# Adding x by an accumulating DMA to rows filled with b_up, four raw slots, and rewritten engine orders, in a role-switched adapter with layer norm

## What is computed

```python
h = einsum('bsh,bhk->bsk', x, W_down[role]) + b_down[role][:, None, :]
h = gelu(h, approximate=False)
u = einsum('bsk,bkh->bsh', h, W_up[role]) + b_up[role][:, None, :]
y = x + u
mean = y.mean(-1, keepdims=True)
var = ((y - mean) ** 2).mean(-1, keepdims=True)
out = (y - mean) * rsqrt(var + 1e-5) * gamma[role][:, None, :] + beta[role][:, None, :]
```

## Time and profile before

| | us |
|---|---|
| three runs | 407.95, 413.99, 415.98 |
| median of the runs | 413.99 |
| span of the profiled execution, first to last instruction | 407.0 |
| busy in it: PE, DVE, ACT, POOL | 369.9, 312.0, 193.2, 163.5 |
| mean granted TensorE clock in it | 0.954 |

### The profile page before, as it was taken

How to read it: one execution, slowest core, us unless ns; L and a number is a source line. 1 busy time by engine, 2 the same in 40 slices (tenths; PEclk the granted TensorE clock), 3 DMA queues, 4 the chain that set the end, 5 groups by cost and what they waited for, 6 DMA issues and landing times.

```text
span 407.0 us, 5068 instructions
## 1 busy us (share of the span) xinstructions
PE 369.9 (91%) x1548; PEld 298.2 (73%) x1548; DVE 312.0 (77%) x262; ACT 193.2 (47%) x358; POOL 163.5 (40%) x138
## 2 busy tenths in 40 slices
PE   6969879988999799997999979997999959999992
PEld 2748668866888678886888868886788848888881
DVE  1899298889776996959877897769969695694475
ACT  3459434584353733565343942637335652353332
POOL 0830195247330863217621473307532164328221
PEclk8799989998999989998999989999899988999998
DMA  6489902698128862399326991287813985244022
GB/s 196 169 306 376 387 16 105 201 394 331 56 103 304 324 248 99 131 330 335 136 103 203 324 392 61 103 294 279 303 75 135 333 263 225 94 157 163 0 103 104
DMA packets 23489, 84.05 MB, mean 206 GB/s; under 512 B 2741, under 2 KB 2741, under 8 KB 23477
## 3 DMA queue, kind: packets, MB, share of 16 engines
q1 hardware_dynamic: 23480, 83.94, 56.4%
HBM read 67.15 MB, written 16.78 MB: 206 GB/s over the span
## 4 chain that ended last, share of the span: by engine, by line
PE 54%; DVE 16%; issue 8%; ACT 8%; DMA 7%; POOL 4%; SPq 1%; ACTq 0%; DVEq 0%; POOLq 0%
PE up_ps L279 32%; PE down_ps L271 22%; DVE wd_lo L485 4%; DVE h_lo L555 4%; DVE x_lo L480 4%; ACT x_hi L349 3%; ACT h_full L408 2%; POOL rows L449 2%; DMA x_stage<-xT 2%; DMA rows<-x 2%; DMA wu_stage<-W_up 2%; DVE rows L497 2%; DMA wd_stage<-W_down 1%; ACT squares L368 1%; DVE rows L526 1%
## 5 line engine op out<-in xcount | busy, mean ns | idle before, releaser
L449 POOL TENSOR_TENSOR rows<-rows,b_up_all 128x1024 f32<-128x1024 f32 x32 | 89.8, 2823 | 135.0 <-DMA rows<-x 109.5
L279 PE MATMUL up_ps<-wu_hi,h_hi 128*128 128x512 f32 x256 | 85.6, 415 | 20.8 <-DVE h_lo L555 16.8
L271 PE MATMUL down_ps<-x_hi,wd_hi 128*128 128x512 f32 x256 | 83.4, 397 | 7.3 <-DVE wd_lo L485 3.5
L279 PE MATMUL up_ps<-wu_lo,h_hi 128*128 128x512 f32 x256 | 83.2, 405 | 0.0
L279 PE MATMUL up_ps<-wu_hi,h_lo 128*128 128x512 f32 x256 | 83.0, 404 | 0.0
L271 PE MATMUL down_ps<-x_lo,wd_hi 128*128 128x512 f32 x256 | 82.3, 393 | 0.0
L271 PE MATMUL down_ps<-x_hi,wd_lo 128*128 128x512 f32 x256 | 81.4, 389 | 0.0
L279 PEld LDWEIGHTS up_ps<-wu_hi,h_hi 128*128 128x128 f32 x256 | 50.2, 200 | 35.2 <-issue 20.9
L480 DVE TENSOR_TENSOR x_lo<-x_stage,x_hi 128x1024 fp32r<-128x1024 f32 x32 | 60.2, 1882 | 9.5 <-ACT x_hi L349 9.5
L497 DVE SCALAR_TENSOR_TENSOR rows<-up_ps,rows 128x1024 f32<-128x1024 f32 x31 | 37.9, 1222 | 37.4 <-PE up_ps L279 29.7
L271 PEld LDWEIGHTS down_ps<-x_hi,wd_hi 128*128 128x128 f32 x256 | 48.6, 191 | 19.2 <-issue 6.8
(11 more groups left out here) (36 smaller groups left out, 288.4 us busy)
## 6 DMA issues: line engine op xcount, KB each, us to landing
x_stage<-xT SPq DMA_DIRECT2D x32, 512.0 KB, 5.8
wu_stage<-W_up SPq DMA_DIRECT2D x32, 512.0 KB, 8.3
rows<-x SPq DMA_DIRECT2D x32, 512.0 KB, 7.7
wd_stage<-W_down SPq DMA_DIRECT2D x31, 512.0 KB, 6.0
out<-rows SPq DMA_DIRECT2D x31, 512.0 KB, 2.6
wd_stage<-W_down SPq DMA_DIRECT2D x2, 256.0 KB, 5.5
out<-rows SPq DMA_DIRECT2D x2, 256.0 KB, 2.0
roles_sb<-roles SPq DMA_DIRECT2D x1, 0.0 KB
```

Of the source, the lines that this page charges most:

```text
L271: return pe.matmul(down_ps[:, kc, :], wd_part[:, n, c * K + kc * P:c * K + (kc + 1) * P], x_part[:, n, c * S:(c + 1) * S], start=start, st ...
L279: mm = pe.matmul(up_ps[:, t % 2, half], h_part[:, kc, t * P:(t + 1) * P], wu_part[:, kc, half], start=(kc == 0 and h_part is h_hi and wu_p ...
L449: pool.tensor_tensor(rows[:, t, :], rows[:, t, :], b_up_all[:, bass.ds(role * H, H)], ALU.add).then_inc(biased, 1)
```

## The change

- `x_stage` and `wd_stage` get a slot for each of the four parts, with a semaphore for each slot. A part of batch b + 1 can be loaded as soon as the same part of batch b is split.
- The first chunk of x is loaded and rounded apart, as the first chunk of W_down was.
- The roles and b_down are loaded from ScalarE's queue instead of SP's.
- b_up, gamma and beta are no longer kept for all roles. In each batch SP fills `rows[:, t, :]` with the role's row of b_up (one DRAM row read for 128 partitions, 512 KB written), four times, and loads `gamma_row` and `beta_row` in the same way.
- x is added to the filled rows by a DMA with `accum_op=ALU.add`, issued by POOL after the fill has landed. The add on POOL and its semaphore `biased` are gone.
- The last tile of a batch is summed, centred, finished and stored at the beginning of the next batch; SP, ScalarE, POOL and VectorE have new orders.
- ScalarE takes the squares of a tile in one instruction, except for the very last tile, and POOL makes rstd in two operations.
- TensorE waits for `summed` one tile less far ahead at t = 0.

The core of the diff:

```diff
-        x_stage = sb("x_stage", [P, NSTAGE, CPL * S], F32)
-        wd_stage = sb("wd_stage", [P, NSTAGE, CPL * K], F32)
+        x_stage = sb("x_stage", [P, NLOAD, CPL * S], F32)
+        wd_stage = sb("wd_stage", [P, NLOAD, CPL * K], F32)
...
+            def load_next_part(b, next_role, i):
+                sp.wait_ge(x_split, NLOAD * b + i + 1)
+                load_x_part(b + 1, i)
+                sp.wait_ge(wd_split, NLOAD * b + i + 1)
+                load_wd_part(next_role, i)
...
+            def fill_rows(b, t, role):
+
+                if not is_first(b):
+                    sp.wait_ge(stored[t], 16 * b)
+                sp.dma_start(rows[:, t, :], b_up[bass.ds(role, 1), :].partition_broadcast(P)).then_inc(b_up_in_rows[t], 16)
+
+            def load_role_row(row, param, role, landed):
+                sp.dma_start(row[:, :], param[bass.ds(role, 1), :].partition_broadcast(P)).then_inc(landed, 16)
...
             def steps(b):
                 first, last = is_first(b), is_last(b)
+                role = load_role(sp, b)
                 if not last:
                     next_role = load_role(sp, b + 1)
...
+                    load_next_part(b, next_role, 0)
+                fill_rows(b, 0, role)
+                fill_rows(b, 1, role)
+                if not first:
+                    store(b - 1, NT - 1)
+                fill_rows(b, 2, role)
+                load_role_row(gamma_row, gamma, role, gamma_landed)
+                load_role_row(beta_row, beta, role, beta_landed)
+                fill_rows(b, 3, role)
                 if not last:
+                    for i in range(1, NLOAD):
+                        load_next_part(b, next_role, i)
                     for i in range(KC):
                         sp.wait_ge(wu_split, KC * b + i + 1)
                         load_wu_part(next_role, i)
...
+                for t in range(NT - 1):
+                    store(b, t)
...
@@ block.tensor @@
                     if t < 2:
                         if not first:
-                            pe.wait_ge(summed, NT * b)
+                            pe.wait_ge(summed, NT * b - 2 + t + 1)
...
@@ block.scalar, steps @@
                 if not first:
+                    variance(b - 1, NT - 1)
                     act.wait_ge(up_ready, NT * b)
...
+                round_wu(b)
+                gelu(b, 0, role)
                 if not last:
...
+                    round_next_part(b, 0)
+                gelu(b, 1, role)
+                gelu(b, 2, role)
+                gelu(b, 3, role)
+                if not last:
+                    round_next_part(b, 1)
+                    round_next_part(b, 2)
+                variance(b, 0)
+                if not last:
+                    round_next_part(b, 3)
+                variance(b, 1)
+                variance(b, 2)
...
@@ block.gpsimd @@
-                    pool.tensor_tensor(rows[:, t, :], rows[:, t, :], b_up_all[:, bass.ds(role * H, H)],
-                                       ALU.add).then_inc(biased, 1)
...
+            def add_rows(b, t):
+                pool.wait_ge(b_up_in_rows[t], 16 * (b + 1))
+                pool.dma_start(rows[:, t, :], x[b, t * P:(t + 1) * P, :], accum_op=ALU.add).then_inc(rows_landed[t], 16)
...
-            for param_row, all_roles, _ in params:
-                pool.partition_broadcast(all_roles[:, :], param_row).then_inc(params_spread, 1)
...
+            for t in range(NT):
+                add_rows(0, t)
+            for t in range(NT - 1):
+                inverse_deviation(0, t)
+            with pool.Fori(1, B) as b:
+                add_rows(b, 0)
+                add_rows(b, 1)
+                inverse_deviation(b - 1, NT - 1)
+                add_rows(b, 2)
+                add_rows(b, 3)
+                for t in range(NT - 1):
+                    inverse_deviation(b, t)
+            last_inverse_deviation()
...
@@ block.vector @@
+            def first_half_steps(b):
+
+                first, last = is_first(b), is_last(b)
+                if not first:
+                    sum_tile(b - 1, NT - 1)
+                    centre_tile(b - 1, NT - 1)
+                    finish_tile(b - 1, NT - 1)
+                split_wu(b)
+                split_h(b, 0)
+                if not last:
+                    split_x_part(b + 1, 0)
+                    split_wd_part(b + 1, 0)
+                for kc in range(1, KC):
+                    split_h(b, kc)
+
+            def steps(b):
+                first_half_steps(b)
+                split_x_part(b + 1, 1)
+                split_wd_part(b + 1, 1)
+                split_x_part(b + 1, 2)
+                sum_tile(b, 0)
+                centre_tile(b, 0)
+                split_wd_part(b + 1, 2)
+                finish_tile(b, 0)
+                sum_tile(b, 1)
+                split_x_part(b + 1, 3)
+                centre_tile(b, 1)
+                split_wd_part(b + 1, 3)
+                finish_tile(b, 1)
+                sum_tile(b, 2)
+                centre_tile(b, 2)
+                finish_tile(b, 2)
```

More of the change, by code:

```diff
@@ L194, in load_wu_part @@
-            def load_wu_part(role, i):
[L195 to L199, removed]
+                sp.dma_start(wd_stage[:, i, :], wd_src(role)[:, i, :]).then_inc(wd_landed[i], 16)
+            def load_next_part(b, next_role, i):
[3 more added lines that the diff above has]
+                load_wd_part(next_role, i)
@@ L201, in steps, with store @@
+            def store(b, t):
+                sp.wait_ge(normed, NT * b + t + 1)
+                sp.dma_start(out[b, t * P:(t + 1) * P, :], rows[:, t, :]).then_inc(stored[t], 16)
             def steps(b):
                 first, last = is_first(b), is_last(b)
+                role = load_role(sp, b)
                 if not last:
                     next_role = load_role(sp, b + 1)
[L205 to L221, removed]
+                    load_next_part(b, next_role, 0)
@@ L225, in steps @@
                         load_wu_part(next_role, i)
[L226 to L237, removed]
+                for t in range(NT - 1):
+                    store(b, t)
+            sp.dma_start(x_stage[:, 0, 0:S], x_src(0)[:, 0, 0:S]).then_inc(first_x_landed, 16)
+            sp.dma_start(x_stage[:, 0, S:CPL * S], x_src(0)[:, 0, S:CPL * S]).then_inc(x_landed[0], 16)
             sp.wait_ge(roles_landed, 16)
             first_role = load_role(sp, 0)
[L240 to L247, removed]
+            sp.dma_start(wd_stage[:, 0, 0:K], wd_src(first_role)[:, 0, 0:K]).then_inc(first_wd_landed, 16)
+            sp.dma_start(wd_stage[:, 0, K:CPL * K], wd_src(first_role)[:, 0, K:CPL * K]).then_inc(wd_landed[0], 16)
+            for i in range(1, NLOAD):
                 load_x_part(0, i)
-                sp.wait_ge(wd_split, i - NSTAGE + 1)
                 load_wd_part(first_role, i)
@@ L256, in _ @@
             steps(B - 1)
+            for i in range(HALVES):
+                sp.wait_ge(normed, NT * B + i)
+                half = slice(i * BANK, (i + 1) * BANK)
+                sp.dma_start(out[B - 1, (NT - 1) * P:NT * P, half], rows[:, NT - 1, half]).then_inc(last_stored, 16)
             for t in range(NT - 1):
@@ L290, in steps @@
                     parts = NLOAD * b + n + 1
[L291 to L295, removed]
+                    chunks_apart = first and n == 0
+                    for down_pass in range(len(PASSES)):
+                        if down_pass == 0 and not chunks_apart:
+                            pe.wait_ge(x_hi_ready, parts)
+                            pe.wait_ge(wd_hi_ready, parts)
+                        elif down_pass == 1:
+                            pe.wait_ge(x_split, parts)
+                        elif down_pass == 2:
+                            pe.wait_ge(wd_split, parts)
                         for c in range(CPL):
-                            if first_chunk_apart:
-                                pe.wait_ge(*((first_chunk_hi, 1) if c == 0 else (wd_hi_ready, 1)))
+                            if chunks_apart and down_pass == 0:
+                                pe.wait_ge(*((first_x_hi, 1) if c == 0 else (x_hi_ready, 1)))
+                                pe.wait_ge(*((first_wd_hi, 1) if c == 0 else (wd_hi_ready, 1)))
                             for kc in range(KC):
@@ L362, in round_next_part, with round_wu, gelu @@
                 round_wd_part(b + 1, i)
[L364 to L369, removed]
+            def round_wu(b):
+                for i in range(KC):
+                    act.wait_ge(wu_landed[i], 16 * (b + 1))
+                    act.copy(wu_hi[:, i, :], wu_stage[:, i, :]).then_inc(wu_hi_ready, 1)
+            def gelu(b, kc, role):
+                act.wait_ge(down_ready, KC * b + kc + 1)
+                if not is_first(b):
+                    act.wait_ge(normed, NT * b)
+                bias = b_down_all[:, bass.ds(role * KC + kc, 1)]
+                act.activation(h_full[:, kc, :], down_ps[:, kc, :], ACT.Gelu, bias=bias).then_inc(h_full_ready, 1)
```

(23 more changed lines are left out.)

213 lines of the change are left out of this document (89 added, 124 removed).

## The result

The changed kernel takes 446.17 us (median of 4 runs, 444.34 to 447.91) against 414.0 (4 runs, 407.95 to 415.98): a ratio of 1.093, 95% interval 1.083 to 1.103. It is slower. The forecast was 378 us in a range of 368 to 412, so both sign and range are wrong; slower had a chance of 0.14. The profiled execution took 445.05 us, its span is 442.9.

What follows compares the result with a forecast made beforehand. TensorE was taken as the bound, delayed by `h_lo` stops. Up matmuls starting last at 338.4 plus a 29.5 us tail give 368, batch 0's stop 374.6, and 3 for scatter 378 us; range 368 to 412.

Steps and rivals of the forecast that it cites:

- What bounds the kernel before: TensorE, 43.5 us a batch, loses 3.8 more to stops for `h_lo`, stretched beside POOL's adds of b_up.
- VectorE's load: VectorE's work per batch after the change: 33 us in a period of 43.5, against 38.7 before.
- D: Start of a batch's down matmuls; up ones start at D+21.8, the next batch at D+43.5.
- Just in time: Tile 0's sum for the next batch ends near D+31.3; TensorE wants the bank at D+32.7.
- With some 3 us of cover: POOL's wait for fills before tile 3's deviation stays hidden: finish at D+11.6, fourth `h_lo` 10.1 us later, wanted at D+25.9.
- rival 3: Tile 3's deviation behind the fills on POOL: slow issues and late fills use up the cover; 409 us, chance 0.10.
- No stop: TensorE wants the fourth `h_lo` at D+25.9; it is ready at D+23.9, 2 us of cover.
- The price of the accumulate: Each accumulating DMA of x taken as two loads, 2.56 us, bounded by 1.28 and 3.84.
- Rival 2: DMA the bound, accumulates reading and writing in turn, from 4.8 us each on; 432 us at 6 us, chance 0.13.
- Rival 1: DMA nearly full: x2 near D+31, sum 1.7 us late, six batches lose some 3.3 each; 403 us, chance 0.20.
- Batch 0: First batch: column blocks end at 33.9, 4.0 us gained; then a 5.2 us stop for the sum, 6.7 with low clock.
- Rival 4: POOL, writing descriptors, stretches VectorE as its adds did, so half of the stops stay; 392 us, chance 0.05.

Runs made afterwards that it cites:

- e7: In the kernel before, POOL adds b_up to one column of 1024 only, all waits kept; 375.56 us, ratio 0.916.
- e10: In the kernel before, VectorE instead of POOL adds b_up, one tile at a time just ahead of each sum; 379.32 us, ratio 0.931.
- e2: Changed kernel with, on POOL, the inverse deviation of the batch before's tile 3 ahead of the two accumulating DMAs; 430.31 us, ratio 1.050.
- e8: Changed kernel with deviation first on POOL and, on SP, fills 0 and 1 before x parts 1 and 2, part 3 behind fill 3; 381.04 us, 0.930.

## Why the prediction was wrong, point by point

**What bounds the kernel before: right.** That the stops on `h_lo` come from POOL's wide adds was shown by e7 and e10, whose period is 43.5. They are worth 3.8 us a batch by the prediction's count and 4.7 by the sums of tile 0 (48.2 before).

**VectorE's load: right.** 33 us a batch were forecast; 250.9 us in eight batches are 31. `h_lo` is at 0.69 throughout.

**The step that failed: the deadlines were checked once, from a D at which everything before was on time.** The prediction let store 2 and part 0 go out "from about D+0.5" and found x2 landed "near D+27.7", the sum ended at "D+31.3" for a wish of D+32.7, and concluded "Just in time". But by these terms the sum starts near D+30.0 (27.7 + 1.05 + 1.22), 29.5 us after store 2. From its start VectorE has three tiles and three splits of parts to do before the next store 2, and at the prediction's lengths that is 3 x (1.22 + 1.31 + 1.29) + 3 x 1.22 = 15.1 us. So by its own terms the ring was 44.6 us long, 1.1 over TensorE's 43.5: each lap starts 1.1 us later against TensorE than the one before, and the slack of 1.4 us is gone in the second. A slack at one deadline says nothing when the start depends on the deadline of the lap before. That should have been a sum around the ring.

That sum alone would have put 6 to 8 us on the forecast. The rest, 9.5 of the 10.6 us between 43.5 and 54.1, is in **terms of the ring that were too small**:

- From store 2's issue to the end of tile 3's finish 14.6 us (123.09 to 137.73) for 11.1. SP issues the first load 2.6 us after the store; the two roles that it reads there weren't priced.
- From tile 3's finish to x2 landed 19.7 (137.73 to 157.4) for 16.1.
- From the sum's start to store 2 17.5 (105.61 to 123.09) for 15.1, which has no wait for a mean or a deviation in it.

44.6 and these 9.5 are the 54.1 of the trace. TensorE's last up matmuls start at 413.34 in the changed kernel, where the prediction had 338.4:

```profile
413.34 21.77 PE up_ps L246 x96
```

The tail behind that start was right: 29.6 us to the end of the span, forecast 29.5.

**"With some 3 us of cover": wrong.** The finish of tile 3 ended at 137.7, 17.0 us after the down matmuls' start at 120.71, for a forecast of D+11.6. Of the 5.4 us more, 1.9 are the later start (store 2 at D+2.4 instead of D+0.5) and 3.5 the longer way from there. So the gelus were late, the sign of rival 3 (58.6 us in the trace), and TensorE waited for `h_lo` 15.9 us in eleven times where "No stop" was forecast. e2, which takes this wait off POOL, won 2.2 us a batch.

**The price of the accumulate: right, 10% low.** 20.4% of 442.9 us over 32 is 2.82 us each, forecast 2.56; the other transfers are at 55.8% of 442.9 over 92.29 MB, 1.40 us for 512 KB, forecast 1.28. So the ratio is 2.0. The rule of the Trainium skill ("Collectives: The Full Stack", section "The bandwidth ceiling"), two read descriptors for one write and the add itself free, agrees with it. A batch has 22 x 1.40 + 4 x 2.82 = 42.1 us of transfers, 97% of TensorE's period, where I had 88%. Rival 2 (DMA the bound, from 4.8 us an accumulate on) didn't happen; it had the right sign and the wrong mechanism. Its 432 us lie nearest to the measured time, by luck: the changed kernel's 76.2% of DMA time is below e8's 89.7%. Rival 1's sign, a stop for a sum in each batch, is what TensorE shows, but its price of 3.3 us a batch was that of one lap as well.

**Fills as dear as a load: right.** With fills, gamma and beta rows among them, the hardware queue's mean is 1.40 us, and 1.43 before (56.4% of 407.0 us over 83.94 MB).

**Batch 0: half right.** The up matmuls started at 29.25, not 33.9. The prediction kept the 17.55 of before for the start of the second part's matmuls; they began at 12.93, since the first chunks landed earlier (W_down's second at 7.5 us instead of 10.5) and the granted clock was 1.00 from 6 to 12 us instead of 0.67. x2's cast began at 47.98 (landing forecast 45.5), and TensorE wanted the bank 4.5 us earlier than forecast, so the stop was 11.19 us instead of 5.2. The 5.2 had a slip in it: 45.5 and the 3.49 of rounding, split and sum are 49.0, not 50, and the stop 4.2.

**Rival 4** didn't happen: no stretch on VectorE.

## What to carry to other kernels

When a program waits in place on several engines, look for the ring: follow one tile's chain until it comes back to itself in the next iteration and add up its length without the engine that is thought to be the bound. If that is over the bound's period, slack at single deadlines is worth nothing, and removing one piece may only lengthen another that shares its queue, as in e2; here two reorderings that alone won 2.2 us a batch and nothing won 7.6 together. And before work is moved off an engine into traffic and waits, try the plain move: one add of 1.2 us a tile on an engine with spare time (e10, ratio 0.931) gave as much as four fills and four accumulates a batch in the best order tried (e8, 0.930).

## What the runs showed of the hardware that was not expected

- POOL needs 0.89 us in the mean to issue an accumulating DMA (SP mostly 0.33 to 0.36 for a plain one), and VectorE's subtractions beside it keep their length: in the changed kernel seven `wd_lo` that overlap such an issue take 1214 to 1218 ns, ten `h_lo` 680 to 694.
- Writing the same row of DRAM to 128 partitions costs the queues no more than a plain load (mean of 512 KB on the hardware queue 1.40 us with 48 such transfers in it, 1.43 without).
- A store of 512 KB lands after 4.88 us with two accumulates in flight and after 8.35 behind parts and fills; 2.6 in the median.
